# Block product as three float32r terms, softmax sums of two row groups in PSUM, LayerNorm statistics of two batches in one instruction

## The reference

```python
x = x + _L0_xattn_ref(_layernorm(x, axis=-1), ctx_1024, Wq, bq, Wkv, bkv, Wo, bo)
x = x + _L0_ffn_ref(_layernorm(x, axis=-1), w_router, w_block)

# cross-attention: q from x, k and v from ctx
scores = jnp.einsum('bhqd,bhkd->bhqk', q, k) / math.sqrt(D)
attn = jax.nn.softmax(scores, axis=2)          # over the QUERIES
out = jnp.einsum('bhqk,bhkd->bhqd', attn, v)

# feed-forward: the 96 of 128 tokens with the highest x @ w_router
processed = jax.nn.gelu(jnp.einsum('bkd,de->bke', selected, w_block))
out = x.at[batch_idx, top_idx].set(processed)  # the other 32 tokens pass through
```

## Time and profile before

| | us |
|---|---|
| median of 3 runs | 921.36 (921.07 to 921.6) |
| span of the profiled execution | 919.4 |
| PE / DVE / ACT / POOL busy | 889.4 / 873.5 / 879.5 / 796.8 |

### The profile page before, as it was taken

How to read it: one execution, slowest core, us unless ns; L and a number is a source line. 1 busy time by engine, 2 the same in 40 slices (tenths; PEclk the granted TensorE clock), 3 DMA queues, 4 the chain that set the end, 5 groups by cost and what they waited for, 6 DMA issues and landing times. The chain is left out here.

```text
span 919.4 us, 31003 instructions
## 1 busy us (share of the span) xinstructions
PE 889.4 (97%) x10306; PEld 753.9 (82%) x10306; DVE 873.5 (95%) x2320; ACT 879.5 (96%) x4503; POOL 796.8 (87%) x1488
## 2 busy tenths in 40 slices
PE   7899999999999999999999999999999999999973
PEld 6788888888888888888888888888888888888861
DVE  6899999999999999999999999999999999999887
ACT  5999999999999999999999999999999999999983
POOL 4568789999989999899999999999899999998865
PEclk9999999999999999999999999999999999999997
DMA  6222123223223223223223223223223222221102
GB/s 198 62 65 71 46 61 95 57 84 93 57 84 95 60 83 92 58 86 91 70 75 91 59 86 91 71 74 89 76 71 89 76 71 87 76 61 53 49 24 92
DMA packets 70976, 70.45 MB, mean 77 GB/s; under 512 B 12064, under 2 KB 62752, under 8 KB 70816
## 3 DMA queue, kind: packets, MB, share of 16 engines
q1 hardware_dynamic: 69456, 67.68, 25.5%
q10 hardware_dynamic: 1360, 0.79, 0.3%
HBM read 35.13 MB, written 16.78 MB: 56 GB/s over the span
## 5 line engine op out<-in xcount | busy, mean ns | idle before, releaser
L567 ACT ACTIVATE e_sb<-ps_s,neg_max 128x128 f32<-128x128 f32 x2048 | 719.1, 411 | 4.4 <-DVE neg_max L712 3.9
L567 ACT ACTIVATION_READ_ACCUMULATOR e_sb<-ps_s,neg_max 128x1 f32 x2048 | 513.5, 251 | 0.0
L712 DVE TENSOR_REDUCE neg_max<-ps_s 128x4 f32<-128x512 f32 x512 | 329.0, 663 | 26.4 <-PE ps_s L337 26.4
L337 PE MATMUL ps_s<-q_eo,k_sb 32*128 32x256 f32 x2048 | 146.6, 400 | 1.1 <-DVE k_sb L790 0.5
L402 PE MATMUL ps_a<-e_sb,v_pad 128*32 128x128 f32 x4096 | 138.4, 276 | 2.2 <-DVE x_sb L729 1.6
L299 PE MATMUL ps_a<-w_o_sb,o_sb 128*128 128x256 f32 x512 | 133.2, 382 | 2.0 <-DVE v_sb L803 1.9
L299 PE MATMUL ps_t<-w_z_sb,xt_sb 128*128 128x258 f32 x512 | 132.6, 381 | 1.3 <-DVE z_sb L815 1.3
L1042 POOL TENSOR_TENSOR v_pad<-v_sb,recip 128x256 f32<-128x256 f32 x128 | 79.6, 622 | 54.0 <-DVE recip L757 52.5
L402 PEld LDWEIGHTS ps_a<-e_sb,v_pad 128*32 128x32 f32 x4096 | 104.1, 109 | 24.0 <-issue 21.6
L337 PEld LDWEIGHTS ps_s<-q_eo,k_sb 32*128 32x128 f32 x2048 | 92.5, 184 | 29.4 <-ACT e_sb L567 17.0
L1031 POOL TENSOR_TENSOR x_sb<-x_sb,bo_sb 128x256 f32<-128x256 f32 x128 | 114.0, 892 | 0.2
(11 more groups left out here) (102 smaller groups left out, 2197.6 us busy)
## 6 DMA issues: line engine op xcount, KB each, us to landing
x_sb<-in_x SPq DMA_DIRECT2D x64, 256.0 KB, 2.9
c_sb<-in_ctx SPq DMA_DIRECT2D x64, 256.0 KB, 3.1
out<-z_sb SPq DMA_DIRECT2D x64, 256.0 KB, 2.4
q_eo<-q_raw SPq DMA_DIRECT2D x504, 32.0 KB, 2.0
z_sb<-in_L_xattn_Wkv ACTq DMA_DIRECT2D x2, 256.0 KB, 7.2
z_sb<-in_L_xattn_Wq ACTq DMA_DIRECT2D x1, 256.0 KB, 4.5
w_z_sb<-in_L_ffn_w_block SPq DMA_DIRECT2D x1, 256.0 KB, 7.6
w_o_sb<-in_L_xattn_Wo SPq DMA_DIRECT2D x1, 256.0 KB, 7.0
```

The source lines that it names most:

```text
L337: mm = nc.tensor.matmul(ps_s[:, bank(b, j), c, :, :], k_sb[rows, r2, c, h * T:(h + 1) * T], q_eo[rows, r2, :, c, h, :], start=True, stop=True)
L567: last = nc.scalar.activation(e_sb[:, b % 4, j, c, par, :], ps_s[:, bank(b, j), c, par, :], ACT.Exp, bias=neg_max[:, b % 4, h:h + 1], accu ...
L712: nc.vector.tensor_reduce(neg_max[:, b % 4, :].rearrange("p (c j q) -> p j c q", c=C, j=J)[:, j, :, :], ps_s[:, bank(b, j), :, :, :], AX.X ...
```

## The change

Four things are changed.

The block product takes its operands as float32r pairs. ScalarE copies the transposed `x1` out of PSUM as `xt_hi` (`x1_high`, new), VectorE subtracts it as `xt_lo` (`x1_low`, in the place of the copy `x1_transposed`), and the block's weights are split once at the start (`block_weights_high` on ScalarE in step 2, `block_weights_low` on VectorE in step 3). TensorE has six float32r matmuls in the place of two float32 ones.

The sums of the groups 2 and 3 go into PSUM, each to the first element of the score block that its exponential has read; those of the groups 0 and 1 stay in SBUF. The reciprocal is split in two: `inverse_sums_23` stands behind `maxima(s, 0)` of the same step, and the next scores on TensorE wait for it; `inverse_sums_01` stands where `inverse_sums` was.

The exponentials of group 0 move behind the step's end on ScalarE: the order becomes `x1_high(s-4)`, two exponentials of group 0 of `s-1`, `attention_copy(s-2)`, the other two, `gelu_tanh`, `inputs_high`, then the groups 3, 2 and 1 of `s`.

A `bn_stats` reads two batches at once, interleaved element by element, so that its even places are one batch and its odd places the other one. It gives mean and squared deviation of both; `bn_aggr` is gone but for the last two batches of the second LayerNorm, and GpSimd scales the squared deviation itself. In the loop both kinds of statistics run in odd steps only, `stats1_of_pair(s + 11)` near the start and `stats2_of_pair(s - 3)` near the end.

```diff
 # TensorE
 def scores(b):
                 if has(b - 1):
+                    pe.wait_ge(recip_23_ready, upto(b - 1))
                     pe.wait_ge(exp_ready[1], upto(b - 1))
 def block_product(b, settled=False):
-                full_terms(ps_z,
-                           lambda c: xt_sb[:, b % 2, c * T:(c + 1) * T],
-                           lambda c: w_z_sb[:, c, :]).then_inc(z_mm, 1)
+                if b == 0:
+                    pe.wait_ge(w_z_lo_ready, 1)
+                three_terms(ps_z,
+                            lambda a, c: (xt_hi, xt_lo)[a][:, b % 2, c * T:(c + 1) * T],
+                            lambda a, c: (w_z_hi, w_z_lo)[a][:, c, :]).then_inc(z_mm, 1)
 # ScalarE
+            def block_weights_high():
+                act.wait_ge(w_z_ready, 1)
+                nc.scalar.copy(w_z_hi[:, :, :], w_z_sb[:, :, :]).then_inc(w_z_hi_ready, 1)
+            def x1_high(b, settled=False):
+                if has(b):
+                    act.wait_ge(xt_mm, upto(b))
+                    nc.scalar.copy(xt_hi[:, b % 2, :], ps_xt).then_inc(xt_hi_ready, 1)
 def exps(b, j, settled=False, halves=range(C)):
                         last = nc.scalar.activation(e_sb[:, b % 4, j, c, par, :], ps_s[:, bank(b, j), c, par, :], ACT.Exp,
                                                     bias=neg_max[:, b % 4, h:h + 1],
-                                                    accum_out=sums[:, b % 4, h:h + 1])
+                                                    accum_out=(ps_s[:, j, c, par, 0:1] if j >= 2 else
+                                                               sums[:, b % 4, c, j, par:par + 1]))
             for s in range(2, B):
                 sure = 20 <= s < B - 1
+                x1_high(s - 4, sure)
+                exps(s - 1, 0, halves=(0,))
                 attention_copy(s - 2, sure)
+                exps(s - 1, 0, halves=(1,))
                 gelu_tanh(s - 7)
                 inputs_high(s + 5, sure)
                 exps(s, 3, sure)
                 exps(s, 2)
                 exps(s, 1)
-                exps(s, 0)
+                if s == 2:
+                    block_weights_high()
 # VectorE
-            def x1_transposed(b, settled=False):
-                    dve.wait_ge(xt_mm, upto(b))
-                    if has(b - 2) and not settled:
-                        dve.wait_ge(z_mm, upto(b - 2))
-                    nc.vector.tensor_copy(xt_sb[:, b % 2, :], ps_xt).then_inc(xt_ready, 1)
+            def x1_low(b):
+                    dve.wait_ge(xt_hi_ready, upto(b))
+                    nc.vector.tensor_tensor(xt_lo[:, b % 2, :], ps_xt, xt_hi[:, b % 2, :].bitcast(f32),
+                                            ALU.subtract).then_inc(xt_ready, 1)
+            def stats2_of_pair(b):
+                if b % 2 == 0 and has(b):
+                    dve.wait_ge(x1_ready, upto(b + 1))
+                    nc.vector.bn_stats(st2[:, pair(b), :],
+                                       x1_sb[:, b % R:b % R + 2, :].rearrange("p q e -> p e q")).then_inc(st2_ready, 2)
+            def stats1_of_pair(b):
+                if b % 2 == 0 and has(b):
+                    dve.wait_ge(x_in[pair(b)], landed(b))
+                    nc.vector.bn_stats(st1[:, pair(b), :],
+                                       x_sb[:, b % R:b % R + 2, :].rearrange("p q e -> p e q")).then_inc(st1_ready, 2)
+            def inverse_sums_23(b):
+                if has(b):
+                    dve.wait_ge(exp_ready[2], upto(b))
+                    nc.vector.reciprocal(recip[:, b % 4, :].rearrange("p (c j q) -> p j c q", c=C, j=J)[:, 2:4, :, :],
+                                         ps_s[:, 2:4, :, :, 0]).then_inc(recip_23_ready, 1)
             for s in range(2, B):
-                x1_transposed(s - 4, sure)
+                x1_low(s - 4)
+                if s == 3:
+                    block_weights_low()
                 if s >= 4:
-                    stats1(s + 10)
-                aggregate2(s - 3)
+                    stats1_of_pair(s + 10 if s == 4 else s + 11)
...
-                if s >= 4:
-                    aggregate1(s + 10)
...
-                inverse_sums(s - 1)
+                inverse_sums_01(s - 1)
...
+                inverse_sums_23(s)
                 final(s - 16, sure)
-                stats2(s - 2)
+                stats2_of_pair(s - 3)
                 product_scaled(s - 4, sure)
 # GpSimd
-                    pool.wait_ge(mv1_ready, upto(b + 1))
-                    nc.gpsimd.tensor_tensor(ve1[:, r], mv1[:, r, 1], eps_sb[:, :], ALU.add).then_inc(ve1_ready, 2)
+                    pool.wait_ge(st1_ready, upto(b + 1))
+                    nc.gpsimd.tensor_scalar(ve1[:, r], m2_1[:, r], 1.0 / E, EPS, ALU.mult, ALU.add).then_inc(ve1_ready, 2)
```

More of the change, by code:

```diff
@@ L555, in weights_high, with exps @@
                                      scale=SCALE if n == "q" else 1.0).then_inc(w_hi_ready[n], 1)
-            def exps(b, j, settled=False):
+            def block_weights_high():
[5 more added lines that the diff above has]
+                    nc.scalar.copy(xt_hi[:, b % 2, :], ps_xt).then_inc(xt_hi_ready, 1)
+            def exps(b, j, settled=False, halves=range(C)):
                 if not has(b):
                     return
[L561 to L564, removed]
+                if 0 in halves:
+                    act.wait_ge(max_ready[j], upto(b))
+                    if j == 3 and has(b - 4) and not settled:
+                        act.wait_ge(a_mm, upto(b - 4))
+                for c in halves:
                     for par in range(2):
@@ L662, in _ @@
             attention_copy(B - 1)
+            x1_high(B - 2)
             gelu_tanh(B - 6)
-            for b in range(B - 13, B - 8):
+            unprocessed(B - 13)
+            unprocessed(B - 12)
+            x1_high(B - 1)
+            for b in range(B - 11, B - 8):
                 unprocessed(b)
@@ L871, in _ @@
             even_odd_mask()
-            for b in range(2):
-                stats1(b)
-                aggregate1(b)
+            stats1_of_pair(0)
             weights_low("q")
-            for b in range(2, 4):
-                stats1(b)
-                aggregate1(b)
+            stats1_of_pair(2)
             weights_low("k")
@@ L882, in _ @@
             query_bias()
-            for b in range(4, 6):
-                stats1(b)
-                aggregate1(b)
+            stats1_of_pair(4)
             inputs_low(2)
@@ L894, in _ @@
             inputs_low(4)
-            for b in range(6, 8):
-                stats1(b)
-                aggregate1(b)
+            stats1_of_pair(6)
             keys(2)
             centre_block_weights()
+            inverse_sums_23(0)
             maxima(1, 3)
@@ L943, in _ @@
                 router(s - 15, 7)
+                inverse_sums_23(s)
                 final(s - 16, sure)
-                stats2(s - 2)
+                stats2_of_pair(s - 3)
                 product_scaled(s - 4, sure)
                 if s < 4:
-                    for b in range(2 * s + 6, 2 * s + 8):
-                        stats1(b)
-                        aggregate1(b)
+                    stats1_of_pair(2 * s + 6)
             router(B - 16, 8)
-            x1_transposed(B - 4)
-            aggregate2(B - 3)
+            x1_low(B - 4)
             router(B - 16, 9)
-            inverse_sums(B - 1)
+            inverse_sums_01(B - 1)
             router(B - 16, 10)
-            x1_transposed(B - 3)
+            x1_low(B - 3)
             product_scaled(B - 4)
@@ L961, in _ @@
             residual(B - 2)
[L962 to L963 removed]
+            stats2_of_one(B - 2)
+            aggregate2_of_one(B - 2)
             final(B - 16)
             final(B - 15)
[L966 removed]
+            x1_low(B - 2)
             gelu_product(B - 6)
             residual(B - 1)
[L969 to L970 removed]
+            stats2_of_one(B - 1)
+            aggregate2_of_one(B - 1)
             product_scaled(B - 3)
[L972 removed]
+            x1_low(B - 1)
             final(B - 14)
```

98 lines of the change are left out of this document (50 added, 48 removed).

## The result

| | before | changed |
|---|---|---|
| median, us | 921.22 (920.96 to 921.6, 4 runs) | 913.84 (912.23 to 914.03, 4 runs) |
| span of the profiled execution, us | 919.4 | 910.4 |

The ratio is 0.9916, with a 95% interval of 0.9903 to 0.9929: 0.8% faster. The time lies in the stated range of 899 to 931, which held the rivals too, but above the 901 to 911 of the forecast as reasoned, and the way there was not one of those forecast. TensorE's block product is shorter by just what was worked out, but more than half of what that is worth was lost again at a place that I had priced at nothing. That the time fell into the wide range is therefore luck.

A forecast was written before the change was run, and what follows sets the result against it. TensorE was taken as the bound at 6.86 us a step, going to 6.73: 125 steps x 0.13 = 16 us off the 919.4 span, plus 1 for ends, 904.4; the median 2.0 above, 906. Range 899 to 931, chance 0.78 to 0.80.

The forecast's parts named there:

- the forecast as reasoned: Whole kernel: steps of 6.69 to 6.77 us give 901 to 911 us, chance 0.50.
- 0.16 less a step: TensorE's block product: six float32r matmuls take 0.71 us in place of 0.87, bringing TensorE's step from 6.86 to 6.70.
- The 0.03 that I added: Step length: 0.03 us on top of TensorE's 6.70 for four nearly full engines that don't mesh freely, giving 6.73.
- Queues of DMAs: Input loads: a pair is read one step earlier relative to its load, but loaded a whole step before; cost nothing.
- 6.47 forecast: ScalarE's load a step: 6.79 with `x1_high`, less 0.32 for eight sums in PSUM at 0.04 us each.
- the backlog of up to 0.14: ScalarE: results come 0.14 us late after 16 exponentials; up to that much more a step if the cast's wait goes.
- my rival's 912.5 to 931: ScalarE becomes the bound at 6.79 to 6.93 us a step as sums in PSUM give nothing back; chance 0.20 for 911 to 931.
- the load before: VectorE before the change: the 6.86 us step less 0.13 of waits for scores, 6.73; forecast to become 6.59.
- The strided read: VectorE rival: interleaved `bn_stats` reads take double time, 0.55 us more a step, 957 us; chance 0.20 for 935 to 965.
- New waits: Scores waiting for reciprocals of groups 2 and 3: nothing while VectorE isn't behind; `x1_low` up to 0.2 us late behind `x1_high`.
- The rival by which the new order holds TensorE up: TensorE: late `x1_low` or reciprocals in router-work steps cost 0.05 to 0.1 us a step, 911 to 918; chance 0.08 for 911 to 920.
- Ends: Start and last steps: splitting the block's weights and passing each `x1` through two engines cost together 1 us more.

The follow-up runs named there:

- the first experiment: The changed kernel with the load of x issued first in SP's loop, ahead of the queries' eight transfers and the store: 902.17 us, ratio 0.9803.

## Why the prediction was right or wrong

**TensorE, right.** 0.16 less a step, matmuls at 0.12, a step of 6.70: all three shown, the last by the first experiment. Undoing it alone (918.08) shows that the gain needs it. The 0.03 that I added because "four engines that near to each other don't mesh for nothing" isn't there: 6.704 measured.

**Queues of DMAs, the step that failed.** "A pair of inputs is read one step earlier relative to its load than now; it is loaded a whole step before, nothing." I took the loop's index for a time. SP's place in its loop says when the issue may come, and eight issues that take 5 to 6 us and a store stand ahead of it. The trace of before has all that is needed. SP's timeline there:

```profile
164.87 4.95 SPq L248 DMA_DIRECT2D q_eo<-q_raw  x8
169.86 0.58 SPq L233 DMA_DIRECT2D out<-z_sb  x1
170.49 0.47 SPq L218 DMA_DIRECT2D x_sb<-in_x  x1
```

and the statistics of the first LayerNorm on VectorE:

```profile
174.05 0.40 DVE L746 BATCH_NORM_STATS2 st<-x_sb 128x6 f32<-128x256 f32 x1
180.76 0.41 DVE L746 BATCH_NORM_STATS2 st<-x_sb 128x6 f32<-128x256 f32 x1
```

By the loops, the load of a pair in step `s` is read first in step `s+3` (`stats1(s + 10)`), and after the change in `s+2` (`stats1_of_pair(s + 11)`). The data of the load at 170.49 are there at 173.4 (2.9 later) and are read at 180.76: 7.4 us of room. One step earlier takes 6.7 of it. About 0.7 us are left, and the eight issues ahead of the load, which take between 5 and 6 us, can use them up. It cost 9.0 us in 104 steps. In the changed kernel the wait adds up to 17.4 us more than with the load first (20.8 less 3.4). VectorE's wait for scores is 3.1 shorter (16.3 against 19.4), and the span 9.2 longer; where the other 5 us were made up is not taken apart.

**ScalarE, direction right, size wrong.** A sum in PSUM shortens the start distance by 0.042 (0.04 forecast). But the room that I drew from it was not there: 6.47 forecast, an estimated 6.67 by the ends' distances and the series of 0, 4 and 8 sums. That a start distance is what an instruction takes up of its engine holds only while the engine gets pauses. I had named the backlog of up to 0.14 and then left it out, "nothing as long as there is room"; eight sums at 0.031 in place of 0.04 are another 0.07. The second part is thus not a reserve but what keeps the first one alive: without it 928.22, inside my rival's 912.5 to 931, whose step of up to 6.93 was measured as 6.92. (The 912.5 left out the 1 us for the ends that stands beside it; with it the sum is 913.7. The changed kernel's 913.84 lies there by coincidence: in its trace TensorE does not wait for ScalarE as it does without the sums in PSUM.)

**VectorE, too high, and it did no harm.** The pair's statistic starts 0.61 ahead of its follower (579.35 to 579.96 on VectorE in the first experiment) where I had 0.59, two reciprocals take 0.22 where I had 0.25, `x1_low` 0.33 (587.05 to 587.38). The terms held; the load before, "6.86 - 0.13 = 6.73", did not, since a busy engine's waits are not all of its room. By that load single statistics would have made steps of 6.83 (6.73, and 0.09 and 0.01 for the reciprocals and `x1_low`); they made 6.70. GpSimd's "at most 6.64", taken from its waits in the same way, is no bound either: in the first experiment it waits for the reciprocals only 1.7 us from 300 to 800 us, 0.02 a step of 6.70.

**The strided read, fell.** 957 us was the price of a doubled read; it costs 0.012 us, and the 0.20 that I gave this rival had no row behind it. The Trainium skill's rule in "SBUF — State Buffer" (Door 1: The DMA port swizzle), that each access to a new line pays, does not show in this read on VectorE: 692 against 680 ns. The measurement decides.

**New waits, small as forecast.** Ahead of the scores in the whole changed kernel TensorE's weight loads wait 4.8 us for the reciprocals and its matmuls 1.4, and `xt_lo` waits for `xt_hi` 3.0 us in 7 times, only 0.7 of it between 100 and 870 us. The rival by which the new order holds TensorE up gave 911 to 918, and the measured time lies there; but its mechanism, late reciprocals or `x1_low`, is not the one that was found.

**Ends.** Of the first experiment's 18.2 us of span, 16.5 fall in the 104 steps, 0.159 a step; 125 such steps would give 19.8, so the ends cost 1.6 where I had 1.

**The sum again.** A span of 904.4 was forecast. 19.8 us off the steps in place of 16 and 0.6 more at the ends bring it to 901.2, where the first experiment is, and the late load adds 9.2: 910.4. So the two misses, the 0.03 too much and the load at nothing, went against each other.

## What to carry to other kernels

When a read moves, take the load's row and the first reader's row from the trace and subtract the landing time: the loop's index is no clock, and a queue that issues in order puts everything ahead of the load into the sum. Read a nearly full engine by the distances of its ends, not of its starts, and don't take its waits for its spare time. And when two parts of a change buy room on engines that aren't the bound, ask of each whether the part that gains needs it: here the sums in PSUM were needed, and the joint statistics cost 9.5 us until the load was moved, and gave nothing clear of noise after it.

## What was unexpected of the hardware

- An exponential with its sum: starts 0.342 and ends 0.349 us apart with the sum in SBUF, 0.300 and 0.319 with it in PSUM. The rows grow from 0.37 to 0.56 us through a step of the changed kernel by that difference. In the kernel with all sums in SBUF, where ScalarE gets no pause, they start out at 0.69.
- `final` on VectorE and an addition on GpSimd, each with two operands in SBUF, hold each other up: 0.82 us in place of 0.48 for `final` when the addition has started 0.18 us ahead of it, 0.92 to 1.07 in place of 0.73 for the addition otherwise.
- `bn_stats` over 512 elements reads interleaved (step 1024 bytes) in 692 ns and contiguous in 680 ns.
- A reciprocal of 8 elements takes 188 ns from PSUM and 187 from SBUF, against 238 for 16 before; from start to start 0.11 against 0.16.
- Eight DMA issues of 32 KB hold SP for 5 to 6 us here, waits for their data included, while one load of 256 KB issues in 0.5 and lands in 2.9 us.
